# A chunked linear-attention scan on four 32x32 squares of TensorE instead of two 64x64 ones

## The reference, cut to what matters

```python
def step(s, inp):
    q_, w_, k_, v_, a_, b_ = inp
    sa = jnp.einsum('bhij,bhj->bhi', s, a_)
    s = s * w_[:, :, None, :] + sa[..., None] * b_[:, :, None, :] + v_[..., None] * k_[:, :, None, :]
    return (s, jnp.einsum('bhij,bhj->bhi', s, q_))
s0 = jnp.zeros((Bx, H, HS, HS), x.dtype)
_, y = jax.lax.scan(step, s0, (qt, wt, kt, vt, at, bt))
```

## Time and profile before

| | us |
|---|---|
| median of the runs | 5526.29 |
| profiled execution, its own time | 5525.3 |
| its span in the trace | 5523.4 |
| the scan's steady part, 240 chunks (1050 to 2230) | 1180 |
| its tail, 16 chunks (2230 to 2312) | 82 |

### The profile page before, as it was taken

One profiled execution on the slowest core, in us unless ns is written; L12 is line 12 of the kernel. 1 busy time (PEld: TensorE's weight loads), 2 busy tenths in 40 slices (PEclk: granted clock), 3 DMA queues, 4 the chain that ended last, 5 costly groups with the idle time before them and its releaser, 6 DMA issues. The chain is left out here.

```text
span 5523.4 us, 194787 instructions
## 1 busy us (share of the span) xinstructions
PE 5133.6 (93%) x70040; PEld 4437.2 (80%) x70040; DVE 3836.5 (69%) x11241; ACT 3332.3 (60%) x9386; POOL 2729.4 (49%) x3833
## 2 busy tenths in 40 slices
PE   6888888699999999666999999999999999999999
PEld 5888888699999999654777777777777777777777
DVE  4666666599999999474666666666666666666665
ACT  4777777255555555354666666666666666666665
POOL 1222222699999999302444444444444444444443
PEclk8999999899999999887999999999999999999999
DMA  2333333566666666492000000000010000000000
GB/s 70 94 94 93 92 94 92 136 149 146 149 144 151 142 149 144 116 292 76 15 15 15 15 15 15 15 15 15 19 48 21 20 21 20 21 20 21 20 21 17
DMA packets 993739, 389.99 MB, mean 71 GB/s; under 512 B 773840, under 2 KB 938448, under 8 KB 992464
## 3 DMA queue, kind: packets, MB, share of 16 engines
q1 hardware_dynamic: 992400, 387.40, 29.0%
q10 hardware_dynamic: 1088, 0.00, 0.0%
HBM read 217.51 MB, written 169.74 MB: 70 GB/s over the span
## 5 line engine op out<-in xcount | busy, mean ns | idle before, releaser
L2248 ACT ACTIVATE l_prob<-l_prob,l_nb,l_rq 128x256 f32<-128x256 f32 x1024 | 604.5, 592 | 275.1 <-DVE l_nb L2034 275.0
L1899 POOL TENSOR_TENSOR l_pn<-l_prob,l_rinv 128x512 f32<-128x512 f32 x512 | 533.0, 1041 | 330.3 <-DVE l_rinv L2014 322.6
L2444 PE MATMUL lD<-l_hid,w 128*128 128x128 f32 x3072 | 388.2, 275 | 19.7 <-DVE l_hid L2089 19.7
L2444 PEld LDWEIGHTS lD<-l_hid,w 128*128 128x128 f32 x3072 | 364.1, 192 | 22.4 <-DVE l_hid L2089 22.2
L2232 ACT COPY l_qT<-lA 128x512 f32<-128x512 f32 x128 | 75.0, 586 | 412.4 <-PE lA L2352 412.4
L1906 POOL TENSOR_TENSOR l_x1s<-l_x 128x128 f32<-128x128 f32 x128 | 58.2, 455 | 516.6 <-DVE l_x L2072 516.4
L1109 POOL TENSOR_TENSOR sc_kT<-sc_tok,sc_headmask 128x128 f32<-128x128 f32 x512 | 299.2, 604 | 0.0
L1217 ACT ACTIVATE sc_d_qk<-sc_part,sc_headmask 128x64 f32<-128x64 f32 x1024 | 270.3, 336 | 38.6 <-DMA sc_part<-scratch_part 38.6
L478 POOL TENSOR_TENSOR rk<-rk,bkraw 128x256 f32<-128x256 f32 x64 | 54.6, 872 | 477.7 <-DVE bkraw L364 477.7
L1109 POOL TENSOR_TENSOR sc_bT<-sc_tok,sc_headmask 128x128 f32<-128x128 f32 x512 | 279.0, 565 | 0.0
L1217 ACT ACTIVATE sc_d_qb<-sc_part,sc_headmask 128x64 f32<-128x64 f32 x1024 | 271.9, 339 | 0.0
(11 more groups left out here) (296 smaller groups left out, 16842.3 us busy)
## 6 DMA issues: line engine op xcount, KB each, us to landing
scratch_cm<-cm SPq DMA_DIRECT2D x64, 512.0 KB, 4.1
sc_early<-scratch_cm SPq DMA_DIRECT2D x128, 256.0 KB, 3.3
scratch_part<-sc_att SPq DMA_DIRECT2D x64, 512.0 KB, 4.5
sc_part<-scratch_part SPq DMA_DIRECT2D x64, 512.0 KB, 4.3
scratch_tok<-vt SPq DMA_DIRECT2D x512, 48.0 KB, 1.8
l_h<-scratch_h SPq DMA_DIRECT2D x128, 129.0 KB, 2.6
scratch_gr<-gr SPq DMA_DIRECT2D x64, 256.0 KB, 2.0
sc_late<-scratch_cm SPq DMA_DIRECT2D x64, 256.0 KB, 3.8
```

The source lines that it names most:

```text
L1899: tt(pn[s][:, pair], prob[s][:, pair], rinv[s][:, pair].unsqueeze(2).broadcast_to([P, 2, 2 * P]), ALU.mult).then_inc(Q["pn"][s].sem, 1)
L2248: last_ = nc.scalar.activation(prob[s][:, h], prob[s][:, h], ACT.Exp, scale=rq8[s][:, h:h + 1], bias=nb[s][:, h:h + 1], accum_out=sums[s][ ...
L2444: last_ = mm(bank[s][3][:, c * P:(c + 1) * P], w2[:, m, c * P:(c + 1) * P], hid[s][:, m], start=(c == 0 and m == 0), stop=(c == CC - 1 and ...
```

## The change

`QH` becomes 32, so a square holds `HQ` = 2 heads and the array is used as four squares on its diagonal. A group becomes 16 products with 32 columns of weights and 32 moving ones. Everything that is expanded to a square's head columns (bx, kx, ax, qx, bT, kT, d_ak, d_t, d_qk, d_qb) is half as long, and ScalarE needs two activations for a diagonal, not four.

TensorE's loop holds two chunks, not four, and the last units are a loop too, with the last two chunks written out; so is the lead-in. What TensorE reads must then depend on the parity of the chunk alone. ax, qx, bT and kT go from four buffers to two, and two copies on ScalarE are new: `aq` (the a and q rows of `early`, 128 elements, behind the copy of Y, for the product of the next chunk's AB) and `vc` (a chunk of v, 64 elements, behind the copy of SA). SyncE's load of v now waits for `v_c`, no longer for Y. GpSimd waits for Y of two chunks before, no longer of four, and does `prepare` ahead of `use`.

```diff
-QH = 64
+QH = 32
@@ buffers
-        ax, qx, bT, kT = ([sb(f"{n}{c}", [P, BG, HQ, CH]) for c in range(UC)] for n in ("ax", "qx", "bT", "kT"))
+        ax, qx, bT, kT = ([sb(f"{n}{c}", [P, BG, HQ, CH]) for c in range(2)] for n in ("ax", "qx", "bT", "kT"))
+        aq, vc = [sb(f"aq{k}", [P, BG, 2 * CH]) for k in range(2)], [sb(f"vc{k}", [P, BG, HS]) for k in range(2)]
@@ SyncE, load_v
-                    sp.wait_ge(S["y_ps"].sem, S["y_ps"].after(first_chunk(w, k) + 2 * j + 1, UC))
+                    sp.wait_ge(S["v_c"].sem, S["v_c"].after(first_chunk(w, k) + 2 * j + 1, UC))
@@ GpSimd, use
-                    pool.wait_ge(S["y_ps"].sem, S["y_ps"].after(n, UC))
+                    pool.wait_ge(S["y_ps"].sem, S["y_ps"].after(n, 2))
@@ TensorE, products
+                    pe.wait_ge(S["aq"].sem, S["aq"].after(m))
-                            for at in halves:
-                                rhs = early[c // 2][at, c % 2, 0, q // CC, q % CC].unsqueeze(1).broadcast_to([QH, 2, 2, CH])
-                                last = mm(bank[at, q * P + x * QH:q * P + (x + 1) * QH], src[c % 2][at, q].rearrange("p h t -> p (h t)"),
-                                          rhs, start=True, stop=True)
+                            for at in tiles:
+                                last = mm(AB_ps[c][at, (2 * q + x) * QH:(2 * q + x + 1) * QH], src[c][at, q].rearrange("p h t -> p (h t)"),
+                                          aq[c][at, q], start=True, stop=True)
@@ TensorE, stacked
-                        for at in halves:
-                            ins = mm(bank[at, q * P:q * P + QH], lhs[at, q].rearrange("p h t -> p (h t)"),
+                        for at in tiles:
+                            ins = mm(bank[at, q * QH:(q + 1) * QH], lhs[at, q].rearrange("p h t -> p (h t)"),
@@ TensorE, the loops
-                with pe.Fori(0, NU - LEAD) as i:
-                    for c in range(UC):
-                        chunk(i, c, True, True)
-                for u in range(NU - LEAD, NU):
-                    for c in range(UC):
-                        chunk(u, c, False, u < NU - 1)
+                with pe.Fori(0, (NU - LEAD) * UC // 2) as i:
+                    for c in range(2):
+                        chunk(2 * i + c, c, True, True)
+                with pe.Fori((NU - LEAD) * UC // 2, NU * UC // 2 - 1) as i:
+                    for c in range(2):
+                        chunk(2 * i + c, c, False, True)
+                for c in range(2):
+                    chunk(NU * UC - 2 + c, c, False, c == 0)
@@ ScalarE
+                def copy_aq(w, k, c):
+                    m = first_chunk(w, k) + c
+                    act.wait_ge(pair["early_in"][c // 2].sem, pair["early_in"][c // 2].after(w * 2 + k))
+                    act.wait_ge(S["ab_ps"].sem, S["ab_ps"].after(m, 2))
+                    nc.scalar.copy(aq[c % 2][:], bg(early[c // 2][:, c % 2, 0].rearrange("p b g y t -> p b g (y t)"))).then_inc(S["aq"].sem, 1)
```

More of the change, by code:

```diff
@@ L889, in scan_stage @@
         Y_ps, AB_ps = ([ps(f"{n}{k}") for k in range(2)] for n in ("Y", "AB"))
-        first16 = lambda bank: bank[:].rearrange("p (q r i) -> p q r i", q=BG, i=HS)[:, :, 0, :]
-        S = signals(nc, ctx, "bk_x ab_ps att_sb ax_x kT_x d_ak d_t d_qk d_qb p_ps p_sb sa_ps sa_sb s_ps s_sum s_sb y_ps y_sb",
+        first16 = lambda bank: bank[:, 0:BG * QH].rearrange("p (q r i) -> p q r i", q=BG, i=HS)[:, :, 0, :]
+        S = signals(nc, ctx, "bk_x aq ab_ps att_sb ax_x kT_x v_c d_ak d_t d_qk d_qb p_ps p_sb sa_ps sa_sb s_ps s_sum s_sb y_ps y_sb",
                     1, "sc", ahead=LEAD)
@@ L1103, in use @@
                         pool.wait_ge(Hf["late_in"][k].sem, Hf["late_in"][k].after(w))
[L1104 to L1106 removed]
+                    pool.wait_ge(S["y_ps"].sem, S["y_ps"].after(n, 2))
+                    expand(ax[c % 2], bg(late[k][:, c, :, :, 0, :]))
+                    expand(qx[c % 2], bg(late[k][:, c, :, :, 1, :])).then_inc(S["ax_x"].sem, 1)
                     for dst, x in ((bT, 0), (kT, 1)):
@@ L1158, in stacked, with value_part @@
                     return ins
-                def value_part(n, c, u):
-                    pe.wait_ge(pair["v_in"][c // 2].sem, pair["v_in"][c // 2].after(u))
+                def value_part(n, c):
+                    pe.wait_ge(S["v_c"].sem, S["v_c"].after(n))
                     pe.wait_ge(S["d_ak"].sem, S["d_ak"].after(n))
@@ L1165, in value_part, with chunk @@
                     pe.sem_inc(s_pass, 1)
[L1166 to L1171, removed]
+                    stacked(P_ps, d_ak[c], vc[c], True, False)
+                def chunk(n, c, more, follow):
+                    s_in, Y = state[c], Y_ps[c]
                     pe.wait_ge(S["ax_x"].sem, S["ax_x"].after(n))
@@ L1185, in chunk @@
                     pe.sem_inc(s_pass, 1)
-                    stacked(SA_ps, d_t[c % 2], p_sb, True, True).then_inc(S["sa_ps"].sem, 1)
+                    stacked(SA_ps, d_t[c], p_sb, True, True).then_inc(S["sa_ps"].sem, 1)
                     pe.wait_ge(S["kT_x"].sem, S["kT_x"].after(n))
                     pe.sem_inc(s_pass, 1)
-                    stacked(S_ps, kT[c], values, True, False)
+                    stacked(S_ps, kT[c], vc[c], True, False)
                     if more:
-                        products(m, c)
+                        products(n + LEAD * UC, c)
                     pe.wait_ge(S["sa_sb"].sem, S["sa_sb"].after(n))
@@ L1196, in chunk @@
                     pe.sem_inc(s_pass, 1)
[L1197 to L1202, removed]
-                pe.wait_ge(s_state, 1)
-                value_part(0, 0, 0)
-                with pe.Fori(0, NU - LEAD) as i:
-                    for c in range(UC):
-                        chunk(i, c, True, True)
-                for u in range(NU - LEAD, NU):
-                    for c in range(UC):
-                        chunk(u, c, False, u < NU - 1)
+                    stacked(Y, d_qb[c], sa_sb, False, True).then_inc(S["y_ps"].sem, 1)
+                    if follow:
+                        value_part(n + 1, 1 - c)
+                with pe.Fori(0, LEAD * UC // 2) as i:
+                    for c in range(2):
+                        products(2 * i + c, c)
+                pe.wait_ge(s_state, 1)
+                value_part(0, 0)
+                with pe.Fori(0, (NU - LEAD) * UC // 2) as i:
[4 more added lines that the diff above has]
+                        chunk(2 * i + c, c, False, True)
+                for c in range(2):
+                    chunk(NU * UC - 2 + c, c, False, c == 0)
             @block.scalar
@@ L1230, in outer, with copy_v @@
                     diagonal(d_qb[c % 2], part[k][:, c, :, 1, :], S["d_qb"])
+                def copy_aq(w, k, c):
[3 more added lines that the diff above has]
+                    nc.scalar.copy(aq[c % 2][:], bg(early[c // 2][:, c % 2, 0].rearrange("p b g y t -> p b g (y t)"))).then_inc(S["aq"].sem, 1)
+                def copy_v(w, k, c):
+                    n = first_chunk(w, k) + c
+                    act.wait_ge(pair["v_in"][c // 2].sem, pair["v_in"][c // 2].after(w * 2 + k))
+                    act.wait_ge(S["y_ps"].sem, S["y_ps"].after(n, 2))
+                    nc.scalar.copy(vc[c % 2][:], v[c // 2][:, c % 2]).then_inc(S["v_c"].sem, 1)
                 def squares(w, k):
@@ L1264, in chunk @@
                     nc.scalar.copy(y[k][:, c], first16(Y_ps[c % 2])).then_inc(S["y_sb"].sem, 1)
+                    if c < UC - 1 and exists(w, k, LEAD):
+                        copy_aq(*shift(w, k, LEAD), c + 1)
+                    if c == UC - 1 and exists(w, k, LEAD + 1):
+                        copy_aq(*shift(w, k, LEAD + 1), 0)
                 act.preload_act_table_set(LN_EXP)
                 act.wait_ge(s_c, 48)
+                for u in range(LEAD):
+                    for c in range(UC):
+                        copy_aq(u // 2, u % 2, c)
+                copy_aq(LEAD // 2, 0, 0)
+                copy_v(0, 0, 0)
                 inner(0, 0, 0)
```

14 lines of the change are left out of this document (7 added, 7 removed).

## The result

The changed kernel takes 5538.51 us (median of 15 runs, 5534.71 to 5544.35), the one before 5526.51 on the same chips: ratio 1.0022, 95% interval 1.0014 to 1.0030. It is slower, by 12 us, where 238 us less was forecast. The forecast and its range both missed.

What follows compares the result with a forecast made beforehand. TensorE, 97% busy, was taken to end last in nearly every chunk. With VectorE last instead, 240 x (4.917 - 4.05) = 208 us, plus tail 26 and lead-in 4, came off, giving 5288 us; range 5205 to 5480.

Steps and rivals of the forecast that it cites:

- TensorE's squares: Groups on TensorE: four squares run side by side, 0.25 us a group, 2.5 us a chunk instead of 4.67.
- three waiting passes: TensorE's issue: it gets past three waiting passes to start the fourth square; two instances of passing one were seen.
- The first rival: TensorE overlaps only two squares, in order: 0.50 us a group, above 5.1 a chunk, 5556 us; chance 0.14.
- the step that failed: GpSimd's expansions take 3.4 us a chunk; waiting for Y of two chunks before costs nothing below 4.05.
- VectorE: VectorE ends last after the change: its shorter d_ak and d_t and less disturbance give 4.05 us a chunk.
- The recurrence: The way from state through P, SA, AB and S back to the state takes 3.1 to 3.3 us, below 4.05.
- SyncE's queue: SyncE's load of v waits for ScalarE's copy rather than for Y, which is earlier; DMA share 0.81.
- Clock, third rival: TensorE gets its lower clock in the steady part: groups 0.43 us, chunk 4.45, 5390 us; chance 0.13.
- ScalarE: hidden: ScalarE: four activations fewer, two copies more, 2.71 us a chunk becomes 1.9; the copies are hidden by its wait for P.
- Tail and lead-in: Last 16 chunks: 82 us become 56, 26 gained; lead-in: shorter expansions, 4 gained.
- The test I had named: If TensorE's idle time in the steady part does not rise to a third or more, the squares step is wrong.

Runs made afterwards that it cites:

- dose: The changed kernel with two more expansions of 128 elements a chunk on GpSimd, written to spare buffers ahead of ax: 5741.50 us.
- the mended kernel: The changed kernel with bx and kx expanded one chunk earlier and four y stores moved behind the loads: 5363.18 us, ratio 0.9711.
- e3: The kernel before, squares still at 64 rows, with prepare ahead of use and GpSimd waiting for Y of two chunks before: 6086.68 us.
- e1: The changed kernel with GpSimd expanding bx and kx one chunk further ahead, before its wait for Y: 5431.84 us, ratio 0.9834.
- a second repair: SyncE's second four y stores of a unit moved behind its first loads; alone in the changed kernel 5528.83 us, ratio 1.0007.

## Why the prediction was wrong, point by point

- **TensorE's squares: right.** Groups at 0.27 us against 0.25 forecast. That TensorE would get past three waiting passes was called an assumption; it held. The first rival (two squares, 5556) came nearest in time, by another mechanism: its groups of 0.50 are not there.
- **GpSimd: the step that failed.** "It now prepares before it uses and may run two chunks ahead instead of four; Y of two chunks before is finished a whole chunk before the expansion is needed. Cost: nothing while 3.4 is below 4.05." Its durations were about right (3.15 us busy a chunk, forecast 3.4). But I asked only when ax is needed, not what is queued behind the wait: bx and kx, on which AB of the same chunk hangs, ahead of S and of the Y that ends the next wait. From the forecast's own terms the ring was there to be summed: 3.4 for the expansions, 0.1 until TensorE starts, four groups of 0.25 and 0.2 to land are 4.7 us, above the 4.05 of VectorE. It measured 3.14, 0.27 and 1.62, so a chunk takes 5.04 us and not 4.05, and the 208 us forecast off the steady part became 29 more. The runs show it by undoing (107 us back), by dose (0.83 for 0.83) and in the kernel before (6087).
- **VectorE: too high.** Expansions 0.365 and 0.388 (forecast 0.44 and 0.48), busy 3.5 us a chunk, not 3.9 (4.05 with its small gaps). Even in the mended kernel it doesn't set most chunks: 0.34 us more on it adds 0.06.
- **The recurrence: too low.** 3.1 to 3.3 forecast, 3.65 measured in the fastest chunks. SA starts 1.09 us behind P, not 0.8, and AB 0.62 behind S, not 0.25; the way through VectorE back to P, 0.58, is as forecast.
- **SyncE's queue: missed.** The load of v was called "earlier". Its condition is; its place, behind four stores, is not, and that was worth 68 us once the ring was open.
- **Clock, third rival:** in part (0.88), with groups of 0.43 as its terms had them. It cost next to nothing, since most of the slow groups run during GpSimd's 3.14 us; a clock of 0.97 took 0.1 off the rest of the turn. With 16 columns it came in full.
- **ScalarE: hidden, as forecast,** though busy 2.2 us a chunk and not 1.9. The copies are near (a and q 0.300, v 0.246, forecast 0.30 and 0.21). The saving was overstated: 0.339 is the mean of records that overlap, while their busy time is 255 us for 960, 0.27 each. **Tail and lead-in:** 16.5 and 3 gained, 26 and 4 forecast.
- **The test I had named** (TensorE idle for a third or more) shows 22%: below it, though the squares were right. Low clock lengthens busy time, so the idle share is a poor test.

Open: what sets each chunk of the mended kernel between 3.65 and 4.6 us, whether a queue order without the late eighth chunk exists, and how much of the ring the order of `prepare` and `use` makes without the wait two chunks back, or the wait without the order; `e3` has both, and `e1` leaves the wait as it is.

## What to carry to other kernels

When a change cuts a buffer's depth or moves a wait on an in-order engine, follow the ring: wait, everything issued behind it, what that releases, and back to the event waited for; if it closes once a chunk, as here, its sum is a lower bound of the chunk, whatever the busy shares. If every engine idles and two wait for each other, look for it and move out what need not be inside. A ring also hides other late things, so a second repair can be worth far more after the first (here 68 us for 8).

## What the runs showed of the hardware

- TensorE starts passes of four squares side by side, 32 records in 0.27 us at a clock of 1.00 and 0.43 at 0.50, if neighbours in the program use different squares; with one square's eight in a row a group takes 0.96 at 0.50.
- With 16 moving columns for 32 the granted clock went from 0.97 to 0.50, though TensorE's records covered 98% of the time and not 86%; a chunk took 0.55 us longer.
- A TensorE loop of 640 products was fetched anew on every turn (712 packets, 11.67 MB, in 60 turns) and ran at 11.6 us a chunk; with 320 in the loop the kernel before fetched 4 packets in 240 chunks.
